# Score products as 128 + 128 + 32 rows in joined groups, and the side products of a stage on other units

## What is computed

```
hidden = concatenate([context, latents], axis=1)             # 1024 + 512 = 1536 rows
q = (latents @ Wq.T)   # 16 heads of 96
k = (hidden @ Wk.T)    # 4 key heads of 96, each for 4 query heads
v = (hidden @ Wv.T)
scores = einsum('bkgqd,bksd->bkgqs', q, k) / sqrt(96)
attn = softmax(scores, axis=-1)
out = einsum('bkgqs,bksd->bkgqd', attn, v)
return out @ Wo.T
```

## Time and profile before

| | |
|---|---|
| median of 3 runs | 1063.67 us (1063.38 to 1064.74) |
| the profiled execution | 1062.25 us |
| its span, first to last instruction | 1060.5 us |
| granted PE clock over the span | 0.999 |
| PE busy | 1038.3 us, 98% |
| POOL, DVE, ACT busy | 644.3, 641.5, 635.6 us |
| the attention, first to last score product | 333.3 to 1019.7 us |

### The profile page before, as it was taken

One profiled execution on the slowest core, in us unless ns is written; L12 is line 12 of the kernel. 1 busy time (PEld: TensorE's weight loads), 2 busy tenths in 40 slices (PEclk: granted clock), 3 DMA queues, 4 the chain that ended last, 5 costly groups with the idle time before them and its releaser, 6 DMA issues.

```text
span 1060.5 us, 18394 instructions
## 1 busy us (share of the span) xinstructions
PE 1038.3 (98%) x7262; PEld 586.4 (55%) x7262; DVE 641.5 (60%) x1092; ACT 635.6 (60%) x711; POOL 644.3 (61%) x348
## 2 busy tenths in 40 slices
PE   9999999999999999999999999999999999998987
PEld 4555444444545556566665655656656565565553
DVE  6989849644223565556556655654655655566767
ACT  5686535431224687665667756657766566677764
POOL 4476778242001589666677865668866667687771
PEclk9999999999999999999999999999999999999999
DMA  9986664843223999999999999899999999999995
GB/s 339 257 306 214 199 212 116 183 81 60 73 88 106 163 214 213 208 214 160 193 179 198 165 234 174 159 210 173 176 214 209 157 195 180 138 177 198 172 195 159
DMA packets 516570, 192.46 MB, mean 181 GB/s; under 512 B 484916, under 2 KB 500148, under 8 KB 516484
## 3 DMA queue, kind: packets, MB, share of 16 engines
q1 hardware_dynamic: 516484, 191.28, 87.5%
HBM read 56.88 MB, written 13.63 MB: 66 GB/s over the span
## 4 chain that ended last, share of the span: by engine, by line
PE 84%; DMA 4%; POOL 4%; DVE 3%; ACT 2%; issue 1%; SPq 1%; DVEq 0%; POOLq 0%
PE ps L556 34%; PE ps L798 20%; PE ps L772 11%; PE ps L813 10%; PE ps L815 5%; DMA region_o<-region_y 1%; DMA ln_t<-stage 1%; DVE p_max L1558 1%; POOL region_y L1723 1%; PE ps L578 1%; POOL x_res L1723 1%; POOL region_c L1723 1%; SPq L517 1%; DMA stage<-ctx_t_in 1%; POOL stage L1723 1%
## 5 line engine op out<-in xcount | busy, mean ns | idle before, releaser
L1723 POOL TENSOR_TENSOR region_y<-p,region_b 128x1536 f16<-128x1536 f32 x128 | 396.9, 3101 | 272.8 <-ACT region_b L1259 257.5
L1249 ACT ACTIVATE p<-ps,p_max 128x1536 f32<-128x1536 f32 x128 | 197.2, 1541 | 197.1 <-DVE p_max L1558 196.9
L1558 DVE TENSOR_REDUCE p_max<-ps 128x1 f32<-128x1536 f32 x128 | 224.9, 1757 | 113.8 <-PE ps L798 113.7
L798 PE MATMUL ps<-region_q,region_c 96*128 96x512 f16 x1152 | 269.8, 379 | 0.0
L813 PE MATMUL ps<-region_q,region_c 128*128 128x192 f16 x1536 | 207.6, 246 | 4.5 <-DVE logit L1583 2.4
L1259 ACT ACTIVATE region_b<-ps,p_max 128x1536 f16<-128x1536 f32 x128 | 196.5, 1535 | 18.5 <-DMA region_c<-region_b 17.8
L815 PE MATMUL ps<-region_q,region_o 128*128 128x96 f16 x1536 | 202.3, 206 | 0.0
L798 PEld LDWEIGHTS ps<-region_q,region_c 96*128 96x128 f16 x1152 | 105.3, 98 | 108.0 <-ACT region_b L1259 0.9
L813 PEld LDWEIGHTS ps<-region_q,region_c 128*128 128x128 f16 x1536 | 150.2, 98 | 23.1 <-issue 4.9
L815 PEld LDWEIGHTS ps<-region_q,region_o 128*128 128x128 f16 x1536 | 150.2, 98 | 13.2
L556 PE MATMUL ps<-region_w,region_q 128*128 128x512 f16 x576 | 134.9, 379 | 2.3 <-DMA region_q<-region_q 1.6
(11 more groups left out here) (151 smaller groups left out, 1152.7 us busy)
## 6 DMA issues: line engine op xcount, KB each, us to landing
stage<-ctx_in SPq DMA_DIRECT2D x16, 512.0 KB, 4.9
stage<-ctx_t_in SPq DMA_DIRECT2D x15, 512.0 KB, 8.7
stage<-wq_in SPq DMA_DIRECT2D x16, 384.0 KB, 4.1
stage<-wo_in SPq DMA_DIRECT2D x16, 384.0 KB, 4.3
k_scratch<-region_o SPq DMA_DIRECT2D x12, 384.0 KB, 6.8
region_q<-k_scratch SPq DMA_DIRECT2D x8, 576.0 KB, 5.9
region_q<-v_scratch SPq DMA_DIRECT2D x8, 576.0 KB, 6.2
x_res<-x_in SPq DMA_DIRECT2D x8, 512.0 KB, 8.8
```

What stands on the lines that cost most here:

```text
L798: ins = nc.tensor.matmul(bank(NSB * (m % 2) + sb_), q_head[0:HD, b, h, hq, qt * P:(qt + 1) * P], k_head[0:HD, b, hk, sb_ * 512:(sb_ + 1) * ...
L1249: nc.scalar.activation(p32[:, m % 2, :], rows, ACT.Exp, bias=p_max[:, m % 4:m % 4 + 1], accum_out=den[:, m % 4:m % 4 + 1]).then_inc(e32_ok, 1)
L1558: nc.vector.reduce_max(p_max[:, m % 4:m % 4 + 1], rows, axis=AX, negate=True).then_inc(max_ok, 1)
L1723: return nc.gpsimd.tensor_tensor(out, a, b, op)
```

## The change

Four things change.

1. **Scores.** The high by high and high by low and low by high products of 96 rows are 288 rows in all. They are laid out anew as 128 + 128 + 32: in each unit six products of 128 rows (two for each bank), and three of 32 rows, one for each bank, each on its own 32 rows (`score_rest`). From m = 2 on, the three of an odd unit are done in front, right behind those of the even unit before it: six products of 32 rows stand together. For this the even unit waits for `e32_ok` of the exponential of the unit before it.
2. **Layout of queries and keys.** Rows 96 to 127 of `q_head` and `k_head`, and `q_rest` and `k_rest`, hold the pieces. ACT writes the high part of a query block twice in one instruction (96x1024 and 32x1024 for 96x512 and 32x512). DVE puts the low part of 96 rows into `q_low`, and then copies 32x512 pieces of it from SBUF to SBUF: five for a block, seven for the third. A new signal `q_set` tells PE. The keys of a stage are loaded in five transfers for one.
3. **Exponential.** `p_hi` is a copy of `p32` rounded to f16, no longer a second exponential from the banks, so the banks are free at `e32_ok`.
4. **Tables.** The query halves go to units 0, 1, 4, 5, 9, 10 and one output product to unit 11 from 12; the units without a side product are 8 and 12.

```diff
-        Q_AT = {4: (0, 0), 5: (0, 1), 8: (1, 0), 9: (1, 1), 10: (2, 0), 11: (2, 1)}
+        Q_AT = {0: (0, 0), 1: (0, 1), 4: (1, 0), 5: (1, 1), 9: (2, 0), 10: (2, 1)}
...
-        WO_AT = {2: 4, 3: 5, 6: 6, 7: 7, 12: 0, 13: 1, 14: 2, 15: 3}
+        WO_AT = {2: 4, 3: 5, 6: 6, 7: 7, 11: 0, 13: 1, 14: 2, 15: 3}
...
                 sp.dma_start(k_head[0:HD, b, :, :], src).then_inc(k_ld[b], 16)
+                src = k_dram[b, HI, g * HD:g * HD + 2 * HP, :].rearrange("(n d) s -> d n s", n=2)
+                sp.dma_start(k_head[HD:P, b, :, :], src).then_inc(k_ld[b], 16)
+                for r in range(NSB):
+                    src = k_dram[b, HI, g * HD + 2 * HP:(g + 1) * HD, r * 512:(r + 1) * 512]
+                    sp.dma_start(k_rest[HP * r:HP * (r + 1), b, :], src).then_inc(k_ld[b], 16)
...
+            def score_rest(m, start):
+
+                b, qt, h = m // UPS % B, m % UPS // G, m % G
+                for r in range(NSB):
+                    rows = slice(HP * r, HP * (r + 1))
+                    ins = nc.tensor.matmul(bank(NSB * (m % 2) + r), q_rest[b][rows, h, qt * P:(qt + 1) * P],
+                                           k_rest[rows, b, :], start=start, stop=not start)
+                return ins
...
-                    pe.wait_ge(k_ld[b], use(t, B))
-                    pe.wait_ge(q_free, 2 * NJ * (t + 1))
+                    pe.wait_ge(k_ld[b], 5 * use(t, B))
+                rest_behind = m < 2 or m % 2 == 0
+                if u < G:
+                    pe.wait_ge(q_set, NJ * t + min(u + 1, NJ))
                 if m >= 2:
-                    pe.wait_ge(exp_ok, m - 1)
-                for n, (hq, hk) in enumerate(((HI, HI), (HI, LO), (LO, HI))):
+                    pe.wait_ge(e32_ok, m - 1)
+                for n in range(2):
                     for sb_ in range(NSB):
-                        ins = nc.tensor.matmul(bank(NSB * (m % 2) + sb_), q_head[0:HD, b, h, hq, qt * P:(qt + 1) * P],
-                                               k_head[0:HD, b, hk, sb_ * 512:(sb_ + 1) * 512], start=n == 0, stop=n == 2)
+                        ins = nc.tensor.matmul(bank(NSB * (m % 2) + sb_), q_head[:, b, h, n, qt * P:(qt + 1) * P],
+                                               k_head[:, b, n, sb_ * 512:(sb_ + 1) * 512],
+                                               start=rest_behind and n == 0, stop=not rest_behind and n == 1)
+                if rest_behind:
+                    ins = score_rest(m, False)
+                    if m >= 2:
+                        if u + 1 < G:
+                            pe.wait_ge(q_set, NJ * t + min(u + 2, NJ))
+                        pe.wait_ge(e32_ok, m)
+                        score_rest(m + 1, True)
                 ins.then_inc(sc_ready, 1)
...
+                    pe.wait_ge(w_split, wq_n((t + 1) // 2) + (RING // 2 if part == 0 else RING))
                     if part != 1:
-                        pe.wait_ge(w_split, wq_n((t + 1) // 2) + RING)
                         side_free(m)
...
-                    nc.scalar.activation(q_head[rows, t % B, h, HI, :], bank(at)[part, :], ACT.Copy, scale=SCALE
+                    both = bank(at)[part, :].unsqueeze(1).broadcast_to((part.stop - part.start, 2, 512))
+                    nc.scalar.activation(q_head[rows, t % B, h, :, :], both, ACT.Copy, scale=SCALE
                                          ).then_inc(q_hi, 1)
...
-                nc.scalar.activation(p_hi[:, m % 2, :], rows, ACT.Exp, bias=p_max[:, m % 4:m % 4 + 1]
-                                     ).then_inc(exp_ok, 1)
+                act.wait_ge(e32_ok, m + 1)
+                copy(p_hi[:, m % 2, :], p32[:, m % 2, :]).then_inc(exp_ok, 1)
...
+                dve.wait_ge(q_hi, 2 * n + 1)
+                low(q_low[0:HD, :], slice(0, HD), own[0:HD, 0, :]).then_inc(q_free, 1)
+                dve.wait_ge(q_hi, 2 * n + 2)
+                slice_hi = last[HP * j:HP * (j + 1), 0, :]
+                low(last[part, j, :] if j < 2 else rest[third, G - 1, :], part, slice_hi).then_inc(q_free, 1)
+                dve.wait_ge(q_free, 2 * n + 1)
+                nc.vector.tensor_copy(own[part, 0, :], q_low[first, :])
+                nc.vector.tensor_copy(own[part, 1, :], q_low[second, :])
+                for r in (first, second, third):
+                    ins = nc.vector.tensor_copy(rest[r, j, :], q_low[third, :])
+                if j == 2:
+                    dve.wait_ge(q_free, 2 * n + 2)
+                    for r in (first, second):
+                        ins = nc.vector.tensor_copy(rest[r, G - 1, :], rest[third, G - 1, :])
+                ins.then_inc(q_set, 1)
```

More of the change, by code:

```diff
@@ L33 @@
 VW = 2 * HD
+HP = 32
 E, R = 3, 40
@@ L98, in flamingo @@
         w_eff = view(region_c, 0, 16384).rearrange("p (h c n) -> p h c n", h=2, c=NC)
-        q_head = view(region_c, 0, 8192).rearrange("p (b g h s) -> p b g h s", b=2, g=G, h=2)
+        q_head = view(region_c, 0, 8192).rearrange("p (b g n s) -> p b g n s", b=2, g=G, n=2)
         pt_hi = view(region_c, 8192, PT * SL).rearrange("p (r n q) -> p r n q", r=PT, n=NS)
         o_tok = view(region_c, 8192 + PT * SL, 2 * QG, F32).rearrange("p (r n) -> p r n", r=2)
+        q_low = view(region_c, 8192 + PT * SL + 4 * QG, QL)
         pt_lo = view(region_o, 0, PT * SL).rearrange("p (r n q) -> p r n q", r=PT, n=NS)
@@ L106, in flamingo @@
         q2 = region_q[:, :]
-        k_head = view(region_q, 0, 4 * SL).rearrange("p (b h s) -> p b h s", b=2, h=2)
-        v_head = view(region_q, 4 * SL, 2 * NS * VW).rearrange("p (b s w) -> p b s w", b=2, s=NS)
-        o_t = view(region_q, 13824, 2 * 2 * QG).rearrange("p (r h j q) -> p r h j q", r=2, h=2, j=NJ)
-        v_last = view(region_q, 13824, 2 * KV * VW).rearrange("p (k t w) -> p k t w", k=KV, t=2)
-        o_cast = view(region_q, 15360, 2 * QG).rearrange("p (h n) -> p h n", h=2)
-        o_part = view(region_q, 16128, HD, F32)
+        k_head = view(region_q, 0, 4 * SL).rearrange("p (b n s) -> p b n s", b=2, n=2)
+        k_rest = view(region_q, 6144, 2 * QL).rearrange("p (b s) -> p b s", b=2)
+        v_head = view(region_q, 7168, 2 * NS * VW).rearrange("p (b s w) -> p b s w", b=2, s=NS)
+        o_t = view(region_q, 11776, 2 * 2 * QG).rearrange("p (r h j q) -> p r h j q", r=2, h=2, j=NJ)
+        v_last = view(region_q, 11776, 2 * KV * VW).rearrange("p (k t w) -> p k t w", k=KV, t=2)
+        o_cast = view(region_q, 13312, 2 * QG).rearrange("p (h n) -> p h n", h=2)
+        o_part = view(region_q, 14080, HD, F32)
+        q_rest = (stage[:, :, 3 * D // 4:D].bitcast(F16),
+                  view(region_q, 14272, G * QL).rearrange("p (g s) -> p g s", g=G))
         y_buf = region_y[:, :].rearrange("p (b d) -> p b d", b=2)
@@ L209, in flamingo @@
         v_ld = [sem(f"v_ld{b}") for b in range(B)]
-        q_ready, q_hi, q_free = sem("q_ready"), sem("q_hi"), sem("q_free")
+        q_ready, q_hi, q_free, q_set = sem("q_ready"), sem("q_hi"), sem("q_free"), sem("q_set")
         sc_ready, max_ok, e32_ok, exp_ok, plo_ok, pv_ok = (
@@ L914, in out_last @@
                     ins.then_inc(wo_ready, 1)
-            pe.wait_ge(exp_ok, NU - 1)
+            pe.wait_ge(e32_ok, NU - 1)
             pe.wait_ge(o_ok, NU - 4)
@@ L926, in _ @@
             out_last(2, 30, 1, (2,))
-            pe.wait_ge(exp_ok, NU)
+            pe.wait_ge(e32_ok, NU)
             expert_mix(5, 3, 0)
@@ L1541, in take_low_q, with low @@
                 t, j = n // NJ, n % NJ
-                for k, (h, rows, part) in enumerate(q_rows(j)):
-                    dve.wait_ge(q_hi, 2 * n + k + 1)
-                    nc.vector.scalar_tensor_tensor(q_head[rows, t % B, h, LO, :], bank(at)[part, :], SCALE,
-                                                   q_head[rows, t % B, h, HI, :], ALU.mult, ALU.subtract
-                                                   ).then_inc(q_free, 1)
+                own, last, rest = q_head[:, t % B, j, :, :], q_head[:, t % B, G - 1, :, :], q_rest[t % B]
+                first, second, third = (slice(HP * r, HP * (r + 1)) for r in range(NJ))
+                part = slice(HD, P)
+                def low(out, rows, hi):
+                    return nc.vector.scalar_tensor_tensor(out, bank(at)[rows, :], SCALE, hi, ALU.mult, ALU.subtract)
+                if n > 0:
+                    dve.wait_ge(q_set, n)
+                dve.wait_ge(q_hi, 2 * n + 1)
[13 more added lines that the diff above has]
+                ins.then_inc(q_set, 1)
             def add_out(at, w):
```

## The result

The changed kernel takes **1148.05 us** (median; 1146.29 to 1148.48), the kernel before 1064.2 beside it: ratio 1.0785, 95% interval 1.0766 to 1.0804. It is slower, as predicted, but by 84 us instead of 22, and outside the range of 1053 to 1126.

The account below looks back on a forecast made before the run. TensorE's own work was taken as the bound, 98% busy, 86.1 us a stage. -41.6 + 35.9 + 28.3 = +22.6 against the median of 1063.67 gave 1086 us, range 1053 to 1126.

Parts of the forecast that it names:

- Part 1: Score products on TensorE: joined 32-row products run three at once, a pair of units takes 3.23 us, -41.6 us in all.
- (C): Rival on the score products: the 32-row products do not overlap, +25 on the forecast, 1111 us; chance 0.12.
- small parts: Banks freed 1.5 us sooner, taken as nothing; key loads 0 to 1 us a stage, taken as 0.
- Part 2: Query block on ScalarE and VectorE: wider query copies and added low-part copies make TensorE wait, +35.9 us.
- -41.6 + 35.9: Score products' saving plus query-block waits, with no copy held by GpSimd: 1058 us.
- Part 3: VectorE's copies against GpSimd: only the third block's sixth and seventh copies are held, seven such blocks, +28.3 us.
- The margin of 0.11 us: How far the fifth copy, at X+1.48, was to start ahead of GpSimd, at X+1.59.
- rival B: VectorE's copies: the first two blocks are held too, 14 more holds of 3.1 us, 1121 us; chance 0.20.
- its last paragraph: A TensorE clock that falls in the waits of over 3 us would add to all outcomes; no size given.

Follow-up runs that it names:

- eighth run: The second run's kernel with the high part again a second exponential out of the banks, TensorE waiting for it: 1089.02 us.
- second run: Changed kernel with all copies kept, but GpSimd's subtraction in a unit with a query block waits until behind the last copy: 1068.32 us.
- eleventh run: Changed kernel with every 32-row copy cut to 128 of 512 columns from the second stage's blocks on: 1100.49 us.
- fourth run: Changed kernel with ten spare TensorE products in front of the wait for the output step, in units behind a query block: 1133.18 us.
- third run: Changed kernel with the copies taken out of the query's block, two made behind each output step: 1100.56 us.
- the fastest kernel: Changed kernel with another side-product table, two copies in the query's block, the others one by one before later output steps: 1049.82 us.

## Why the prediction was right and wrong

**The bound and Part 1 were right.** TensorE's own work was the bound, and the pair costs 3.22 us against 3.23 stepped. The three products of 32 rows overlap fully: a group takes 0.22, not the 0.28 estimated from the 3.07 times of the Trainium skill's page TensorE: Matmul & The Clock Gate (Part 3). The rival in which they don't (C) is out. The earlier release of the banks, taken as nothing in the small parts, is a condition of the joining: without it 21 us are lost (eighth run). Taking it as nothing did no harm, since the change has both, but the reason given was too short.

**Part 2 was near in the middle stages and 10 us too low in all.** Without copies, the even stages behind stage 0 take 82.4 to 83.0 us and the odd ones 84.6 to 85.6. TensorE's work in a stage is now 86.1 - 8 x 0.66 = 80.8. So the waits are 1.6 to 2.2 and 3.8 to 4.8 us, where 2.7 and 4.9 were stepped with the copies' own time in them. X, the end of the second query copy, came at 544.01 + 2.05 = 546.06, that is 5.57 behind the scores' issue at 540.49, against 5.62. The second run, with all copies made and none held, is 4 us above the kernel before; -41.6 + 35.9 had given 6 below. From the kernel before to that run, stage 0 was stepped at +4.2 us and measured +7.7 (82.7 to 90.3), stages 1 to 6 together -8.4 and -4.6, the last stage to the end -1.5 and +1.6. In stage 0 the waits stepped at 3.0, 2.0 and 2.8 were 3.3, 2.5 and 3.3, and a fall of the clock stands behind the first (1.7 us). In stages 1 to 6 GpSimd's delay of 0.8 us in two blocks and 1.4 in the third is part of the difference; what the last stage lost stays open.

**Part 3 had the right mechanism and the wrong blocks.** The step that failed is "so they come every 0.21 us: the fifth starts at X+1.48", together with GpSimd's start at "X+1.59". The length was right (0.285 measured, 0.295 taken). The overlap of 0.085, read from instructions of 1024 values in the earlier trace rows, isn't there between these copies: they come every 0.295 us (546.71, 547.00, 547.30). In the first block of a stage, GpSimd starts at X+1.45, since the high part begins 0.09 before the query copy's modelled end, and the fourth copy comes at X+1.54, 0.09 late. In the other two GpSimd starts at X+1.59, as stepped, but the first copy only at X+0.76 instead of X+0.64, and the fourth at X+1.65, 0.07 late. With either pair of starts, the fifth would have been late at 0.21 too, by 0.04 and 0.01. The margin of 0.11 us was smaller than the error of the spacing (4 x 0.085) and of either start (0.14 and 0.12), and the whole of the first two blocks stood on it. With 0.40 on one side of that margin and 0.20 on the other, the chances were set as if it were safe. This is rival B, word for word: copies over 3 us in every block, stages over 92 us (95.1 to 104.6).

Of the rule in the Trainium skill's page SBUF — State Buffer (Who interferes with whom; a VectorE copy in a mode that uses both ports and a GpSimd instruction exclude one another for the whole instruction) the second and the eleventh run show VectorE's side: copies of 0.28 us when GpSimd comes later, held to its end when it comes first. Which mode the copies ran in, and whether GpSimd waits in its turn, no run here shows.

**Rival B's price was too low.** It gave 1121 for 14 more holds, "less what other waits then overlap". Measured is 1148. The fourth run shows where at least 15 of these 27 us are: in TensorE's clock, which falls at the long waits. An estimate from the trace of the changed kernel is enough for all 27: 14 falls of 1.7 us are 24 in stages 1 to 6, and in stage 0 the lower level lasts 15 us in all past the ends of the waits, 7 us more. The prediction names that in its last paragraph and gives it no price, and no end of the range holds it; this is why the range missed. A block with a hold costs 80 / 21 = 3.8 us instead of 3.1: 73 / 21 = 3.5 us of held copies, and the clock. The 73 and the clock's share together are more than 80, so part of a hold is covered by other waits or given back in the second run, where GpSimd is late; how much is not separated.

**The sum, term by term.** Predicted -41.6 + 35.9 + 28.3 = +22.6. Measured against the kernel before: +4 for the first two terms with nothing held (second run), +80 for the holds with their clock.

## To carry to other kernels

Where a step depends on which of two engines comes first, don't put the likeliest case on a margin of tenths of a us: price both sides as one coin, and look for the order that makes the question void (one wait on GpSimd was worth 80 us). A hold that can't be avoided costs next to nothing if it stands where its engine would wait anyway (47 held copies in the fastest kernel); look for that place in the timeline before moving work, since a hold behind the output step of a crowded unit moved the next maximum by its full 3.4 us. And any mechanism that makes TensorE wait several us needs a second price, that of the clock behind it, here 1.7 us a fall.

## What the runs showed of the hardware

- Copies of 32 rows, SBUF to SBUF in f16, one behind another without a wait: 512 values take 0.285 us and come every 0.295, 128 values take 0.184 and come every 0.197. So of each copy 0.16 us doesn't depend on its length ((0.295 - 0.197) / 384 = 0.26 ns a value). Unlike the f32 instructions in the earlier trace rows, they show no overlap.
- A copy that comes 0.07 to 0.09 us after GpSimd's start waits for the end of that instruction and ends 0.14 us behind it, 3.15 to 3.17 in all; in the third run 0.01 us after is enough (3.23). One that comes 0.01 to 0.03 us ahead passes in 0.185 (eleventh run). Between two GpSimd instructions one waiting copy gets through, and the next waits for the second (3.15, then 1.63 us).
- Three products of 32 rows on different rows of the array start about 3 ns apart and take the time of one; a change between 128 and 32 rows costs 0.10 us each way.
- Behind 14 of the 18 waits of 2.46 to 4.89 us in stages 1 to 6, TensorE's clock was at the lower level for 3.4 us. In stage 0, with waits of 6.2, 5.4 and 7.5, it was there for 6.8, 6.8 and 10.2, and fell before the wait had ended.
